# Attention's mix of the values: three f16 products in place of one f32 product

## The reference

```
h    = x + softmax((ln(x) Wq' + bq) (ctx Wk')' / sqrt(512)) (ctx Wv' + bv) Wo' + bo
ln2  = ln(h)
e    = argmax(softmax(ln2 Wg + bg))                       # per row
out  = h + gelu(ln2 W1[e] + b1[e]) W2[e] + b2[e]
```

## Time and profile before

| | |
|---|---|
| time, median of 3 runs | 449.97 us (446.6 to 453.7) |
| the profiled execution's own time | 449.57 us |
| its span, first to last instruction | 447.8 us |
| mean granted TensorE clock | 0.982 |
| TensorE matmul busy | 403.6 us, 90% |
| VectorE / ScalarE / GpSimd busy | 326.2 / 248.4 / 241.4 us (73 / 55 / 54%) |

### The profile page before, as it was taken

How to read it: one execution, slowest core, us unless ns; L and a number is a source line. 1 busy time by engine, 2 the same in 40 slices (tenths; PEclk the granted TensorE clock), 3 DMA queues, 4 the chain that set the end, 5 groups by cost and what they waited for, 6 DMA issues and landing times.

```text
span 447.8 us, 8731 instructions
## 1 busy us (share of the span) xinstructions
PE 403.6 (90%) x2035; PEld 222.2 (50%) x2036; DVE 326.2 (73%) x655; ACT 248.4 (55%) x568; POOL 241.4 (54%) x305
## 2 busy tenths in 40 slices
PE   6989999997999998878968999999899989999970
PEld 2566665565777766555423444444344434444430
DVE  0276748796577786978869888887887978888650
ACT  1251116678888887755644865555455555556630
POOL 4005916501048887377686366665667675676730
PEclk9999999999999998998998999999999999999997
DMA  8999799912635677237686977788788788898510
GB/s 259 234 389 400 251 396 389 381 64 92 242 97 189 189 260 266 88 96 221 198 259 210 291 239 232 236 233 233 222 238 259 225 244 251 239 244 271 154 50 0
DMA packets 77961, 101.11 MB, mean 226 GB/s; under 512 B 9057, under 2 KB 49005, under 8 KB 76134
## 3 DMA queue, kind: packets, MB, share of 16 engines
q1 hardware_dynamic: 69646, 80.74, 58.5%
q0 software_dynamic: 6400, 19.65, 12.1%
q10 hardware_dynamic: 1880, 0.31, 0.4%
HBM read 70.80 MB, written 31.28 MB: 228 GB/s over the span
## 4 chain that ended last, share of the span: by engine, by line
PE 50%; DVE 18%; issue 9%; DMA 8%; ACT 7%; SPq 3%; POOL 2%; another core or an unknown queue 0%; POOLq 0%; ACTq 0%; DVEq 0%
PE bank L1524 18%; PE bank L1527 9%; PE bank L1459 4%; PE bank L1311 4%; PE bank L1366 3%; PE bank L1475 3%; DMA work<-hidden_blocks 3%; DVE expert_weights L1005 3%; DMA expert_weights<-in_x 2%; PE bank L1451 2%; ACT expert_weights L769 2%; DVE work L1218 2%; SPq L537 2%; DVE expert_weights L1149 2%; DVE ey_bias_split_then_geluT L1223 1%
## 5 line engine op out<-in xcount | busy, mean ns | idle before, releaser
L1524 PE MATMUL bank<-expert_weights 128*128 x312 | 73.8, 379 | 8.0 <-issue 3.8
L1524 PE MATMUL bank<-expert_weights,ey_bias_split_then_geluT 128*128 x312 | 74.6, 382 | 6.6 <-DVE ey_bias_split_then_geluT L1223 6.4
L722 POOL DMA_INDIRECT out_x<-keys_values_then_rows_b x39 | 41.8, 1072 | 69.8 <-DVE keys_values_then_rows_b L1229 58.9
L904 ACT ACTIVATE work<-work,b_columns 128x128 f32<-128x128 f32 x156 | 50.0, 390 | 27.6 <-DVE work L1218 17.9
L898 ACT ACTIVATE work<-bank 128x512 f32<-128x512 f32 x37 | 22.0, 596 | 59.8 <-PE bank L1527 54.9
L1524 PEld LDWEIGHTS bank<-expert_weights 128*128 128x128 f16 x312 | 30.5, 98 | 47.4 <-issue 14.3
L1524 PEld LDWEIGHTS bank<-expert_weights,ey_bias_split_then_geluT 128*128 128x128 f16 x312 | 30.6, 98 | 44.3 <-issue 10.2
L1218 DVE STREAM_TRANSPOSE work<-work 128x512 f32<-128x512 f32 x37 | 42.6, 1150 | 11.0 <-DMA work<-hidden_blocks 6.7
L685 POOL DMA_INDIRECT routed_rows<-work,slot_index x32 | 32.9, 1029 | 29.4 <-DVE slot_index L1094 22.1
L769 ACT ACTIVATE expert_weights<-expert_weights 128x512 f16<-128x512 f32 x56 | 33.9, 625 | 25.3 <-DVE expert_weights L1005 19.7
L1223 DVE TENSOR_TENSOR ey_bias_split_then_geluT<-work,ey_bias_split_then_geluT 128x512 f16<-128x512 f32 x39 | 30.1, 772 | 22.6 <-ACT ey_bias_split_then_geluT L911 19.6
(11 more groups left out here) (198 smaller groups left out, 719.1 us busy)
## 6 DMA issues: line engine op xcount, KB each, us to landing
expert_weights<-in_L_ffn_W SPq DMA_DIRECT2D x14, 1024.0 KB, 10.1
keys_values_then_rows_b<-routed_rows SPq DMA_DIRECT2D x39, 258.0 KB, 3.4
hidden_blocks<-work SPq DMA_DIRECT2D x37, 256.0 KB
work<-hidden_blocks SPq DMA_DIRECT2D x37, 256.0 KB
expert_weights<-in_x SPq DMA_DIRECT2D x16, 512.0 KB, 9.1
expert_weights<-in_x SPq DMA_DIRECT2D x24, 256.0 KB, 3.1
work<-routed_rows SPq DMA_DIRECT2D x72, 64.0 KB
key_bias_then_xn<-routed_rows SPq DMA_DIRECT2D x68, 64.0 KB
```

The source lines that it names most:

```text
L722: pool.indirect_dma_start(out_rows, ids_of, rrow[t.buf][:, 0:D], None, bounds_check=T - 1, oob_is_err=False).then_inc(out_sent[t.buf], 16)
L904: nc.scalar.activation(hid_turned[:, P * c:P * (c + 1)], hid_turned[:, P * c:P * (c + 1)], ACT.Gelu, bias=b1_cols[:, :, :].rearrange("p e ...
L1524: mm(o, a[:, c, :], w_split[:, bass.ds(first + (2 * c + h) * D, D)], start=(c == 0 and h == 0 and not begun), stop=False)
```

## The change

The values, the gate columns and the transposed probabilities are held as f16 halves, and the mix is three f16 products for the gate columns and three for the values.

- Values: VectorE writes the f32 value rows of batch `b` to one of two scratch buffers (`val_full`, in `work`), then does its three `low`, then waits for ScalarE's high half (`value_high(b)`, after each third `high`) and subtracts to get the low half. Both halves take the place of the f32 values in `kv`. The scratch buffer of `b` waits for the low half of `b-2`.
- Gate columns: two small VectorE instructions after `val_gate`.
- Probabilities: `pT` becomes a copy to f16, a wait for it, and a subtraction from the same PSUM bank.
- TensorE enters the attention loop behind two more waits (`val_low`, all eight low halves, and `gate_parts`); GpSimd waits for `val_low` before it writes row numbers into `work`.
- The wait for the pad rows' DMA moves from VectorE's last value copy to ScalarE's last high half.

```diff
--- before.py
+++ after.py
@@ -162,6 +162,7 @@
         bias_area = sb("key_bias_split_then_geluT", [P, B * P])
         bias_rows = bias_area[0:BIAS_LO + 1, 0:B * P // 2].bitcast(F16)
         val_gate = sb("value_gate_columns", [K, B * EM])
+        gate_split = sb("value_gate_split", [K, 2, B * EM], F16)
         split_area = sb("key_bias_then_xn2", [P, B * P])
         key_bias = split_area[0:1 + EM, :]
         b_stage = bias_area[0:BIAS_ROWS, 0:D]
@@ -230,7 +231,10 @@
         xn = work[:, rest:rest + D]
         xnT = [work[:, rest + D * n:rest + D * (n + 1)].rearrange("p (c t) -> p c t", c=C) for n in (1, 2)]
         prob = [work[:, rest + 3 * D + P * n:rest + 3 * D + P * n + K] for n in range(2)]
-        probT = [work[0:K, rest + 3 * D + 2 * P + P * n:rest + 3 * D + 2 * P + P * (n + 1)] for n in range(2)]
+        values = kv[:, 0:2 * B * D].bitcast(F16)
+        val_full = [work[0:K, D * n:D * (n + 1)] for n in range(2)]
+        probT = [work[0:K, rest + 3 * D + 2 * P + P * n:rest + 3 * D + 2 * P + P * (n + 1)].bitcast(F16).rearrange("k (h t) -> k h t", h=2)
+                 for n in range(2)]
         ctx_nat = work[:, 0:B * D].rearrange("p (b n) -> p b n", b=B)
@@ -293,6 +297,10 @@
         ld = {n: sem(f"loaded_{n}") for n in ("wv", "wo", "wg", "bias", "bo", "bg")}
         ctx_half = [sem(f"ctx_half_{h}_loaded") for h in range(2)]
         wkq_in = [sem(f"wk_wq_chunk_{c}_loaded") for c in range(C)]
+        val_high = sem("values_hi_done")
+        val_low = sem("values_lo_done")
+        gate_parts = sem("value_gate_parts")
+        pT_high = sem("probsT_hi_copied")
         w_early = [sem(f"expert_{e}_loaded") for e in range(NEARLY)]
         w_late = sem("expert_6_loaded")
         w_last = [sem(f"last_expert_chunk_{n}_loaded") for n in range(NW)]
@@ -655,6 +663,7 @@
             pool.wait_ge(pre_mm, NJOBS)
             pool.wait_ge(pre_dve, copies("dve"))
+            pool.wait_ge(val_low, B)
             link(nc.gpsimd.iota(ids, pattern=[[P, U]], base=0, channel_multiplier=1))
             def scale(c, n, g):
@@ -810,11 +819,21 @@
                      bank[n % 8][0:1 + EM, 0:4 * K].rearrange("p (b k) -> p b k", b=4), 1.0 / WSCALE)
             act.wait_ge(pre_act, copies("act", J_KB + 1))
             nc.scalar.activation(bias_rows[0:1, :], key_bias[0:1, :], ACT.Copy).then_inc(bias_parts, 1)
+            def value_high(b):
+
+                act.wait_ge(pre_dve, copies("dve", J_VAL + b))
+                if b == B - 1:
+                    act.wait_ge(pad_out, 16 * (E + 1))
+                nc.scalar.activation(values[0:K, (4 * b + 2) * D:(4 * b + 3) * D], val_full[b % 2], ACT.Copy)\
+                    .then_inc(val_high, 1)
+
             def high_of(e):
                 act.wait_ge(w_early[e], 32)
                 for n in range(e * NW, (e + 1) * NW):
                     high(n)
+                    if n % 3 == 2:
+                        value_high((n - (NEARLY - 3) * NW) // 3)
             high_of(NEARLY - 3)
             high_of(NEARLY - 2)
@@ -1041,6 +1060,11 @@
             nc.vector.tensor_tensor(val_gate[:, :].rearrange("p (b e) -> p b e", b=B),
                                     bank[n % 8][0:K, 0:B * (1 + EM)].rearrange("p (b e) -> p b e", b=B)[:, :, 1:1 + EM],
                                     vg_bias[0:K, :].unsqueeze(1).to_broadcast([K, B, EM]), ALU.add).then_inc(pre_dve, 1)
+            dve.wait_ge(pre_dve, copies("dve", J_VG))
+            nc.vector.tensor_copy(gate_split[:, 0, :], val_gate[:, :]).then_inc(gate_parts, 1)
+            dve.wait_ge(gate_parts, 1)
+            nc.vector.tensor_tensor(gate_split[:, 1, :], val_gate[:, :], gate_split[:, 0, :], ALU.subtract)\
+                .then_inc(gate_parts, 1)
             dve.wait_ge(bias_parts, 1)
             nc.vector.tensor_tensor(bias_rows[BIAS_LO:BIAS_LO + 1, :], key_bias[0:1, :], bias_rows[0:1, :], ALU.subtract)\
                 .then_inc(bias_parts, 1)
@@ -1048,12 +1072,14 @@
             for b in range(B):
                 n = J_VAL + b
                 ready(n)
-                if b == B - 1:
-                    dve.wait_ge(pad_out, 16 * (E + 1))
-                nc.vector.scalar_tensor_tensor(kvb[0:K, b, 1, :], bank[n % 8][0:K, :], 1.0 / WSCALE,
+                need(dve, val_low, b - 1)
+                nc.vector.scalar_tensor_tensor(val_full[b % 2], bank[n % 8][0:K, :], 1.0 / WSCALE,
                                                val_bias[0:K, :], ALU.mult, ALU.add).then_inc(pre_dve, 1)
                 for m in range(3):
                     low((NEARLY - 3) * NW + 3 * b + m)
+                dve.wait_ge(val_high, b + 1)
+                nc.vector.tensor_tensor(values[0:K, (4 * b + 3) * D:(4 * b + 4) * D], val_full[b % 2],
+                                        values[0:K, (4 * b + 2) * D:(4 * b + 3) * D], ALU.subtract).then_inc(val_low, 1)
             dve.wait_ge(ld["bg"], 16)
@@ -1107,7 +1133,10 @@
                 dve.wait_ge(pt_done, t + 1)
                 need(dve, pv_done, t - 1)
-                nc.vector.tensor_copy(probT[j % 2], bank[4 + j % 2][0:K, 0:P]).then_inc(pT_done, 1)
+                nc.vector.tensor_copy(probT[j % 2][:, 0, :], bank[4 + j % 2][0:K, 0:P]).then_inc(pT_high, 1)
+                dve.wait_ge(pT_high, t + 1)
+                nc.vector.tensor_tensor(probT[j % 2][:, 1, :], bank[4 + j % 2][0:K, 0:P], probT[j % 2][:, 0, :],
+                                        ALU.subtract).then_inc(pT_done, 1)
             def mixed(c, t, j, turn):
@@ -1442,6 +1471,8 @@
             pe.wait_ge(pre_act, copies("act"))
             pe.wait_ge(pre_dve, copies("dve"))
             pe.wait_ge(bias_parts, 2)
+            pe.wait_ge(val_low, B)
+            pe.wait_ge(gate_parts, 2)
             def transpose_x(t, j):
                 pe.wait_ge(xn_ready, t + 1)
@@ -1471,9 +1502,13 @@
                 pe.wait_ge(pT_done, t + 1)
                 need(pe, x1_done, 2 * t - 2)
-                mm(bank[4 + j % 2][:, P:P + EM], probT[j % 2], val_gate[:, bass.ds(b * EM, EM)], start=True, stop=True)
-                mm(bank[6 + j % 2][:, :], probT[j % 2], kv[0:K, bass.ds(b * (2 * D) + D, D)], start=True, stop=True)\
-                    .then_inc(pv_done, 1)
+                for u, v in PARTS:
+                    mm(bank[4 + j % 2][:, P:P + EM], probT[j % 2][:, u, :], gate_split[:, v, bass.ds(b * EM, EM)],
+                       start=(u + v == 0), stop=(u == 1))
+                for u, v in PARTS:
+                    last = mm(bank[6 + j % 2][:, :], probT[j % 2][:, u, :], values[0:K, bass.ds(b * (4 * D) + (2 + v) * D, D)],
+                              start=(u + v == 0), stop=(u == 1))
+                last.then_inc(pv_done, 1)
             def rank(n, g):
```

## The result

| | before | after |
|---|---|---|
| time, median | 449.08 us (446.6 to 453.7, 4 runs) | 459.22 us (457.87 to 466.21, 4 runs) |
| ratio to before | | 1.0235, 95% interval 1.0167 to 1.0303 |
| profiled execution, its span | 449.57, 447.8 us | 457.87, 456.1 us |
| mean granted TensorE clock | 0.982 | 0.962 |

The change costs 10 us. The forecast was +7.0, and slower by over 2% had a chance of 0.31.

The account below looks back on a forecast made before the run. TensorE was taken to bound the feed-forward and set the loop's early pace, VectorE to bound the changed preparation. Preparation 6.8, clock 1.3 and loop -1.1 gave +7.0 on 449.57: 456.6 us, range 448 to 463.

Parts of the forecast that it names:

- Preparation, +7.2 less 0.4: Before the loop: VectorE's added subtractions release TensorE 7.2 us later; ScalarE's first copy comes 0.4 sooner; sum +6.8.
- The clock, +1.3 (0 to 2.5): Loop start: after idling 8.6 us TensorE starts at 1.2 GHz, making the first steps 1.3 us dearer.
- TensorE, 0.23 us a tile (0.20 to 0.29): Loop mix: f16 value products save 0.23 us a tile, the gate part nothing; a cycle of 2.60.
- VectorE, +0.33: Loop, per tile: pT's copy, drain and subtraction cost VectorE 0.33 us more (0.28 to 0.40).
- Tiles 0 to 7, -1.6: First loop tiles: TensorE bound, VectorE has room, so 7 x 0.23 gives -1.6 us.
- Tiles 8 to 15, -0.8: Middle loop tiles: VectorE binds locally against 0.4 us of slack; 0.1 us a tile gained, -0.8.
- the first rival: VectorE bounds the whole loop: +2.6 us in tiles 8 to 15, +4.0 in the last twelve; 462.7 us, chance 0.22.
- Tiles 16 to 20, -0.2: Loop: ScalarE's wait for the last expert's first chunk swallows gains; -0.2 us from the load's earlier start.
- Late, +1.5: Loop from tile 20 on: pT on the chain of waits costs +0.66 us, the last tiles +0.8.
- The loop together, -1.1: Whole attention loop: -1.6 - 0.8 - 0.2 + 1.5 = -1.1 us, bounds -5 to +5.

Follow-up runs that it names:

- run 3: Changed loop with the old preparation: VectorE writes the values' f16 high half, the low products read it again; 450.21 us, ratio 1.0026.
- run 4: Kernel before, f32 mix kept, plus the change's preparation and waits, with nothing reading the halves; 463.12 us, ratio 1.0336.
- run 1: The changed kernel again, unaltered; 459.85 us, ratio 1.0265.
- run 9: Kernel before, with GpSimd's scaling of every next group between the third and fourth scatter of the current one; 455.02 us, ratio 1.0012.
- run 8: Changed kernel, value halves straight from PSUM, bias added by TensorE, second group's scaling between the first group's second and third scatter; 461.33 us, ratio 1.0214.
- run 10: Changed kernel, halves from PSUM, last batch's halves ahead of two weight halves, every next group's scaling between third and fourth scatter; 457.0 us, ratio 1.0161.
- run 11: run 10's kernel with the scaling one scatter further ahead, between the second and third; 455.44 us, ratio 1.0089.
- run 12: run 11's kernel with the high and low half of the last expert's first weight chunk made one tile later; 451.62 us, ratio 1.0166.
- run 6: run 3's kernel with GpSimd's scaling of the second group between the second and third scatter of the first; 450.17 us, ratio 0.9986.
- run 5: Changed kernel with 32 products added on TensorE between its last value job and the wait for the value halves; 460.78 us, ratio 1.0173.

## Why the prediction was right

The direction, the place of the loss and its size were right (+7.0 for +8.3 in the profiled executions, +10.1 in the medians). That the size came so near is in part luck. Preparation, clock and loop measured +6.6, +3.1 and +0.2, together +9.9; the traced execution shows +8.3 because its stages ahead of the first value job and behind mix 31 were 1.5 us shorter, stages that the change doesn't touch. Inside the loop, tiles 8 to 15 were 3.5 us worse than forecast and the last tiles 2 us better. The bounds that the prediction gives for its own terms add up to 453.5 to 462, not 460; its range doesn't depend on that.

- *Preparation, +7.2 less 0.4.* Measured +6.9 from first value job to first transpose, and ScalarE's answer to it 0.3 sooner (idle 0.84 for 1.16). VectorE is the bound of the stage and the two gate subtractions are hidden, as forecast. Runs 3 and 4 show that this part, with the clock behind it, carries the whole loss.
- *The clock, +1.3 (0 to 2.5).* Too small. From first transpose to mix 0 it is 9.84 us for 7.09; with ScalarE's 0.3 that is 3.1 us, since two tiles' scores and three tiles' transposes ran at half clock and not one or two. In run 1, where one tile's scores and two tiles' transposes are slow, it is 1.7. Both fit a start at 1.2 GHz; how long that lasts differs from run to run. Run 9 has a price without the change: up to mix 0 it does what the kernel before does, its second transposes and the scores behind them ran at half clock, and from first transpose to mix 0 it takes 8.41 us for 7.09, 1.3 more.
- *TensorE, 0.23 us a tile (0.20 to 0.29).* Measured 0.36: 0.29 in the value part, so the gap behind the f32 mix went too, and 0.06 in the gate part that was taken as nothing. By the rule that was weighed (the Trainium skill, TensorE: Matmul & The Clock Gate, section LDWEIGHTS), the three gate products would be 0.32 us. Their three loads do span 0.29 us, but they begin at 122.50, under the transpose before, and the products start 0.08 us ahead of the value products: the trace agrees with how long a load takes, and not with paying for it in full.
- *VectorE, +0.33.* Measured 0.53 - 0.20 = 0.33.
- *Tiles 0 to 7, -1.6.* Mix 0 to 7: -1.8.
- *Tiles 8 to 15, -0.8: the step that failed.* It read 0.4 us of slack a tile on VectorE as the only reserve. Mix 7 to 15 is +2.7 us (run 1: +1.7). The ring over GpSimd, which the prediction doesn't have, binds first: 8.1 us from slot numbers to logits and 3.6 on to the next slot numbers, 11.8 in all, fitted 11.3 us of four f32 tiles plus the picking and ranking, and not 9.9. Runs 8, 10, 11 and 12, which shorten it, have 53.4 to 54.6 us from mix 0 to 19 for 55.6 to 57.5 (run 6, which changes the first group alone, doesn't gain: 58.0); run 9 shows that it didn't bind before. Behind it VectorE binds, as run 10's busy times show, and that is the first rival in its place: it gave +2.6 for these tiles, near the +2.7, though its cause stood second. Its other +4.0, for the last tiles, didn't come.
- *Tiles 16 to 20, -0.2.* Measured -0.2, ScalarE's idle time before the chunk's high half 2.67 for 1.92, as forecast (its row names no releaser in the changed kernel; in run 1 it is 2.21, and the load is named).
- *Late, +1.5.* Mix 20 to 31: -0.5 in the changed kernel, +2.2 in run 1. Within the noise of that stage.
- *The loop together, -1.1.* +0.2 and, in run 1, +1.0. Even with the ring shortened and the chunk moved it is -1.6. The saving of 11 us on TensorE is real, and VectorE, the ring and the late stage leave it no place to show.

**Open.** No run took `pT`'s 0.33 us out alone, so that VectorE binds behind the ring is read from traces and not tested. The price of the half clock in the changed kernel was not taken out alone, since run 5's clock fell too. What sets mixes 19 to 31 beyond the chunk is not settled. Of the 1.8 us between the medians' 10.1 and the traces' 8.3, the 1.5 above may be the most.

## What to carry to other kernels

Before costing a faster operation, look for every ring that runs past it through other engines, and compare its length with the new cycle: a ring that just fits shows next to no wait in the old profile, so its slack must be read as start times (when the result was ready, when it was taken), not as waits. Then compare every engine's whole work a tile with the new cycle: here VectorE's grew by nearly as much (0.33 us) as TensorE's shrank (0.36). Splitting an f32 operand into halves isn't free where each tile uses it, and dear where it is made: if the stage that makes it has two engines full, each added pass is paid in full, and the engine that waits for it may start its next stage at half clock. A sum can be near while its terms are not; check the stages one by one.

## What the runs showed of the hardware

- VectorE and GpSimd got in each other's way: three `low`, with two inputs in SBUF, took 2.45 us beside GpSimd's subtraction and 2.07 without. The first of them starts at 108.33, and GpSimd ends at 107.69 + 1.16 = 108.85; 0.5 of waiting and then three at 0.61 to 0.69 give 110.8, where they end. VectorE's copy out of PSUM, with one SBUF input, kept its 0.68 us under the same GpSimd instruction. This agrees with the Trainium skill (SBUF — State Buffer, section Who interferes with whom): a VectorE instruction with two SBUF inputs contends with a GpSimd instruction that reads SBUF, and the shared port pair is an exclusive lock; one with a single SBUF input, outside the modes that use both ports, doesn't contend.
- The clock did not follow the idle time alone. With the same preparation in the kernel before and in run 9, and the same idle times to 0.02 us (1.42 and 1.16), the second transposes of the loop ran at 0.63 in the kernel before and in run 3, and at 1.09 in run 9, whose rows these are (instructions in order of time):

```profile
105.60 0.63 PE L1461 MATMUL bank<-identity,work 128*128 128x128 f32 x4 [1.42 <-issue]
107.39 1.09 PE L1461 MATMUL bank<-identity,key_bias_then_xn 128*128 128x128 f32 x4 [1.16 <-ACT work L845]
```

  The price is in the clock term above. The Trainium skill (TensorE: Matmul & The Clock Gate, section What's actually happening) says that the monitor's window runs freely and doesn't start with the work, which would explain it; no run here tests that.
